# Normalised context: DMA transpose in place of TensorE transposes, with the layernorm's scale and bias moved into the weights

## What is computed

```python
xn = layernorm(ctx, ln1_w, ln1_b)          # context, 32 x 375 x 256
ln = layernorm(_layernorm(x), ln2_w, ln2_b)
q = (ln @ Wq) per head * (1 + fside) + fside
k, v = split(xn @ Wkv)                     # 16 heads of 64
out = softmax(q @ k.T / 8) @ v @ Wout
x = x + tanh(g_xattn) * out
x = x + tanh(g_ffn) * bitlinear(gelu(bitlinear(_layernorm(x), w1, b1)), w2, b2)
```

## Time and profile before

| | |
|---|---|
| median of 3 runs | 1112.73 us (1112.56 to 1113.78) |
| profiled execution, its time | 1112.75 us |
| its span, first to last instruction | 1110.3 us |
| TensorE matmul (PE) busy | 1063.3 us, 96% |
| weight loads (PEld) | 731.0 us, 66% |
| ScalarE (ACT) busy | 969.6 us, 87% |
| VectorE (DVE) busy | 943.7 us, 85% |
| GpSimd (POOL) busy | 772.5 us, 70% |
| DMA packets of the SP queue | 65.3% of 16 engines' span |

### The profile page before, as it was taken

The page is one execution under the profiler, slowest core; times in us unless marked ns, Lnnn a source line. Parts: engine busy times, 40 slices in busy tenths (PEclk is TensorE's granted clock), DMA queues, the critical chain, the costliest instruction groups (busy, mean ns, idle before and its releaser), DMA issues.

```text
span 1110.3 us, 32139 instructions
## 1 busy us (share of the span) xinstructions
PE 1063.3 (96%) x11910; PEld 731.0 (66%) x11910; DVE 943.7 (85%) x2113; ACT 969.6 (87%) x1867; POOL 772.5 (70%) x838
## 2 busy tenths in 40 slices
PE   3899999999999999999999999999999999999995
PEld 2566667666676666767667667666767667677663
DVE  5797788988888889888988878988888988888886
ACT  5887799999999889999999979999999997999873
POOL 3666667786677767676777766777676777768752
PEclk9899999999999999999999999999999999999998
DMA  8457567666767665679755676755768755765571
GB/s 272 86 106 114 94 102 135 99 110 120 116 119 127 114 101 126 115 111 130 120 98 125 117 107 119 119 101 125 111 120 124 122 98 113 118 113 122 115 124 43
DMA packets 408153, 129.08 MB, mean 116 GB/s; under 512 B 389792, under 2 KB 402848, under 8 KB 408000
## 3 DMA queue, kind: packets, MB, share of 16 engines
q1 hardware_dynamic: 408000, 127.03, 65.3%
HBM read 26.71 MB, written 3.67 MB: 27 GB/s over the span
## 4 chain that ended last, share of the span: by engine, by line
PE 75%; ACT 10%; DMA 5%; issue 4%; POOL 2%; DVE 2%; POOLq 1%; DVEq 1%; ACTq 0%
PE work L872 14%; PE work L873 13%; PE work L874 13%; PE ps_s L891 11%; DMA pt<-pn 5%; PE ps_o L872 3%; PE ps_o L874 3%; PE ps_o L873 3%; ACT prob L618 3%; ACT L618 2%; ACT q_f L584 2%; PE work L955 2%; PE work L997 2%; PE work L946 2%; PE work L968 2%
## 5 line engine op out<-in xcount | busy, mean ns | idle before, releaser
L452 POOL TENSOR_TENSOR pn<-prob,pn 112x750 f16<-112x750 f32 x256 | 399.2, 1565 | 111.5 <-ACT pn L628 100.0
L618 ACT ACTIVATE prob<-ps_s,neg_max 112x375 f32<-112x375 f32 x512 | 264.6, 572 | 10.4 <-DVE neg_max L779 8.6
L779 DVE TENSOR_REDUCE neg_max<-ps_s 112x2 f32<-112x750 f32 x256 | 237.8, 929 | 21.1 <-PE ps_s L891 21.0
L872 PE MATMUL ps_o<-v_h,pt 128*128 128x65 f16 (+1 forms) x1536 | 166.1, 194 | 10.5 <-DMA pt<-pn 8.1
L872 PE MATMUL work<-z,wkv_h 128*128 128x375 f16 x512 | 168.0, 328 | 2.7 <-POOL z L473 2.5
L701 DVE SCALAR_TENSOR_TENSOR k_l<-work,k_h 128x375 f16<-128x375 f32 x256 | 136.4, 541 | 37.9 <-ACT k_h L540 37.8
L540 ACT ACTIVATE k_h<-work 128x375 f16<-128x375 f32 x256 | 121.4, 487 | 53.0 <-PE work L874 48.6
L874 PE MATMUL work<-z,wkv_l 128*128 128x375 f16 x512 | 166.8, 326 | 0.0
L873 PE MATMUL work<-z,wkv_h 128*128 128x375 f16 x512 | 166.5, 325 | 0.0
L873 PE MATMUL ps_o<-v_l,pt 128*128 128x65 f16 (+1 forms) x1536 | 165.9, 192 | 0.0
L874 PE MATMUL ps_o<-v_h,pt 128*128 128x65 f16 (+1 forms) x1536 | 165.8, 193 | 0.0
(11 more groups left out here) (144 smaller groups left out, 2717.7 us busy)
## 6 DMA issues: line engine op xcount, KB each, us to landing
ctx_in<-in_ctx SPq DMA_DIRECT2D x32, 375.0 KB
pt<-pn SPq DMA_TRANSPOSE x256, 3.5
x_in<-in_x SPq DMA_DIRECT2D x32, 112.0 KB, 3.8
x_res<-in_x SPq DMA_DIRECT2D x28, 128.0 KB, 5.0
out<-y SPq DMA_DIRECT2D x28, 128.0 KB, 2.0
stage<-in_wkv SPq DMA_DIRECT2D x2, 1024.0 KB, 9.6
stage<-in_w SPq DMA_DIRECT2D x2, 1024.0 KB, 13.3
stage<-in_wq SPq DMA_DIRECT2D x1, 1024.0 KB, 8.7
```

The costliest lines, as they stand in the source:

```text
L452: g.tensor_tensor(buf[:, 1, :, 0:SK], prob[:, p % 2], buf[:, 0, :, 0:SK], ALU.subtract).then_inc(p_lo, 1)
L618: i = a.activation(prob[:, p % 2, h, :], ps_s[0:SQ, 2 * (p % 2) + h, 0:SK], ACT.Exp, bias=neg_max[:, 2 * (p % 2) + h:2 * (p % 2) + h + 1])
L779: v.tensor_reduce(neg_max[:, 2 * (p % 2):2 * (p % 2) + 2], ps_s[0:SQ, 2 * (p % 2):2 * (p % 2) + 2, 0:SK], X, ALU.max, negate=True).then_in ...
L872: t_.matmul(dst, sh, mh, start=(n == 0), stop=False)
```

## The change

- `Z0`, `Z1`, `ZF0`, `ZF1`, `ZS0`, `ZS1` are gone. GpSimd splits `ctx_n` as it lies, 125 rows by 768, into fp16 halves `zt` (ZC), and one DMA transpose a batch (ZD, issued by SP) turns both into `z`, now in tiles of 128 columns of which 125 are used.
- The layernorm's scale goes into the key and value weights when they are split. Its bias times the key weights (BK) becomes the bias of the key casts, KH and KL, which also lose their constant 1/64 (key weights are scaled by 8, and the query's factors are divided by 8). Its bias times the value weights (BV) times the output weights (BR) becomes one row that a matmul of ones adds in each WO.
- All three key tiles have 125 keys, so the casts and splits of the probabilities write six runs of 125.
- The four small layernorm loads are issued ahead of the key weights. `deq1` has two buffers.
- All lists are written anew. In the repeated round TensorE has:

```diff
+    ("Q0", 0), ("A2", -1), ("A3", -1), ("K5", 0), ("S7", -1), ("K6", 0), ("K7", 0), ("V02", 0),
+    ("S0", 0), ("S1", 0), ("V00", 0), ("A4", -1), ("V01", 0), ("A5", -1), ("K0", 1), ("Q1", 0),
+    ("S2", 0), ("S3", 0), ("ZX", 1), ("K1", 1), ("A6", -1), ("A7", -1), ("OO0", -1), ("V10", 0),
+    ("S4", 0), ("V11", 0), ("K2", 1), ("A0", 0), ("K3", 1), ("OO1", -1), ("S5", 0), ("S6", 0),
+    ("F0", -2), ("V12", 0), ("F1", -2), ("A1", 0), ("WO", -1), ("F2", -3), ("K4", 1),
```

GpSimd and SP:

```diff
+    ("PL2", 1), ("LNA", 3), ("ZXS", 2), ("PL3", 1), ("XB", -1), ("PL4", 1), ("ZC", 3), ("PL5", 1),
+    ("RM2", -1), ("QS0", 2), ("PL6", 1), ("PL7", 1), ("RM1", 0), ("HQ", -1), ("PL0", 2), ("QS1", 2),
+    ("PL1", 2), ("XQ", 0),
...
+    ("ST", -1), ("T4", 2), ("LX", 5), ("T5", 2), ("T6", 2), ("T7", 2), ("HD", 0), ("RS", 2),
+    ("T0", 3), ("XD", 1), ("T1", 3), ("T2", 3), ("T3", 3), ("LD", 6), ("ZD", 5),
```

The rest, cut to its core:

```diff
+            def turn_context(b):
+                sp.wait_ge(z_split, b + 1)
+                if b > 1:
+                    sp.wait_ge(full[BANK[LAST_Z_USER[b - 2]]], USE[LAST_Z_USER[b - 2]])
+                sp.dma_start_transpose(z[b % 2][:].rearrange("p a t c q -> p (a t c) q"),
+                                       zt[:].rearrange("p a t d -> p (a t d)")).then_inc(z_turned, 16)
...
+            def split_context(b):
+                pool.wait_ge(ctx_normed, b + 1)
+                if b > 0:
+                    pool.wait_ge(z_turned, 16 * b)
+                g.tensor_copy(zt[0:TP, 0], ctx_n[:])
                 pool.drain()
+                g.tensor_tensor(zt[0:TP, 1], ctx_n[:], zt[0:TP, 0], ALU.subtract).then_inc(z_split, 1)
...
+            def split_normed_hi(n, loaded, scale, w, hi_part):
+                act.wait_ge(loaded, 16)
+                for k in range(KC):
+                    i = a.activation(hi_part[:, k], w[:, k], ACT.Identity, scale=lnw1s[:, scale, k:k + 1])
...
-                    hi((name, b), job, k_h[:, int(name[2]), :], work[:, BANK[job], 0:SK])
+                    a.activation(k_h[:, c, :], work[:, BANK[job], 0:SK], ACT.Identity, bias=bias_k[:, c:c + 1]).then_inc(hi_done, 1)
...
-                    lo((f"KH{c}", b), job, k_l[:, c, :], work[:, BANK[job], 0:SK], k_h[:, c, :])
+                    v.scalar_tensor_tensor(out=k_l[:, c, :], in0=work[:, BANK[job], 0:SK], scalar=bias_k[:, c:c + 1], in1=k_h[:, c, :],
+                                           op0=ALU.add, op1=ALU.subtract).then_inc(evacuated[BANK[job]], 1)
...
-                    pe.wait_ge(z_ready, 2 * b + 2)
+                    pe.wait_ge(z_turned, 16 * (b + 1))
...
+                    i = three(w[:, 0:SK].rearrange("p (t q) -> p t q", t=TT),
+                              [(wkv_h[:, k, c], wkv_l[:, k, c], zb[:, 0, :, k, 0:TP], zb[:, 1, :, k, 0:TP]) for k in range(KC)])
...
+                if name in ("BK", "BV"):
+                    first = INNER * (name == "BV")
+                    for c in range(IC):
+                        for k in range(KC):
+                            i = t_.matmul(w[:, c:c + 1], wkv_f[:, k, first + c * P:first + (c + 1) * P], lnb1[:, k:k + 1],
+                                          start=(k == 0), stop=(k == KC - 1))
+                if name == "BR":
+                    for c in range(IC):
+                        i = t_.matmul(w[0:QUARTER + 1, 0:D], bias_v[:, c, :], wout_f[:, c, :], start=(c == 0), stop=(c == IC - 1))
...
-                if name in ("Z0", "Z1"):
-                    pe.wait_ge(ctx_normed, b + 1)
-                    c = int(name[1])
-                    for t in range(TT):
-                        i = t_.transpose(w[:, t * TP:(t + 1) * TP], ctx_n[:, t, c * P:(c + 1) * P], ident[0:TP, 0:TP])
...
+                    t_.matmul(w[:, 0:D], bias_ones[:], bias_row[:], start=True, stop=False)
                     for c in range(IC):
-                        t_.matmul(w[:, 0:D], oh, wout_h[:, c, :], start=(c == 0), stop=False)
+                        t_.matmul(w[:, 0:D], oh, wout_h[:, c, :], start=False, stop=False)
```

More of the change, by code:

```diff
@@ L224 @@
     BANK[job], USE[job] = n % WORK_BANKS, n // WORK_BANKS + 1
+FIRST_KEY_HALF = [s[0] for s in sequence("ACT") if s[0] in ("WKH0", "WKH1")][0]
 GELU_COUNT = [t + 1 if t < NT - 1 else t + 2 for t in range(NT)]
 LAST_HALVES = [int(s[0][2]) for s in sequence("DVE") if s[0] in ("HE0", "HE1") and s[1] == NT - 1]
+LAST_Z_USER = [[s for s in sequence("PE") if s[0][0] in "KV" and s[1] == b][-1] for b in range(B)]
 HI_COUNT = {s: n + 1 for n, s in enumerate(s for s in sequence("ACT") if s[0][0:2] in ("KH", "VH"))}
@@ L291, in build @@
         xc, xr, xq = sb("xc", [P, D]), sb("xr", [P, D]), sb("xq", [P, D], F16)
-        amax1, clip1, inv1, qs1, deq1 = (sb(n, [P, 1]) for n in ("amax1", "clip1", "inv1", "qs1", "deq1"))
+        amax1, clip1, inv1, qs1 = (sb(n, [P, 1]) for n in ("amax1", "clip1", "inv1", "qs1"))
+        deq1 = [sb(f"deq1_{i}", [P, 1]) for i in range(2)]
         xqt = sb("xqt", [P, KC, P], F16)
@@ L565, in step @@
                 if name[0:2] == "KH":
-                    hi((name, b), job, k_h[:, int(name[2]), :], work[:, BANK[job], 0:SK])
+                    if b == 0:
+                        act.wait_ge(evacuated[BANK["BK", 0]], USE["BK", 0])
+                    c = int(name[2])
+                    act.wait_ge(full[BANK[job]], USE[job])
+                    a.activation(k_h[:, c, :], work[:, BANK[job], 0:SK], ACT.Identity, bias=bias_k[:, c:c + 1]).then_inc(hi_done, 1)
+                if name == "BRH":
+                    job = ("BR", 0)
+                    act.wait_ge(full[BANK[job]], USE[job])
+                    a.activation(bias_row[:], work[0:QUARTER + 1, BANK[job], 0:D], ACT.Identity, scale=W_SCALE).then_inc(bias_hi, 1)
                 if name[0:2] == "OH":
@@ L585, in step @@
                     i.then_inc(evacuated[BANK[job]], 1)
-                if name in ("ZF0", "ZF1"):
-                    c = int(name[2])
-                    if b == 0:
-                        act.wait_ge(ln_in, 16 * 4)
-                    act.wait_ge(full[BANK[job]], USE[job])
-                    a.activation(zf[:, c, :], work[:, BANK[job], 0:SK], ACT.Identity, bias=lnb1[:, c:c + 1],
-                                 scale=lnw1[:, c:c + 1]).then_inc(evacuated[BANK[job]], 1)
                 if name == "ZXF":
@@ L672, in split_lo, with split_normed_lo @@
                 i.then_inc(lo_split[n], 1)
-            def split_z_first():
-                dve.wait_ge(evacuated[BANK["Z1", 0]], USE["Z1", 0])
-                v.tensor_copy(z[0][:, 0, 1], zf[:, 1])
-                dve.drain()
-                v.tensor_tensor(z[0][:, 1, 1], zf[:, 1], z[0][:, 0, 1], ALU.subtract).then_inc(z_ready, 1)
+            def split_normed_lo(n, scale, w, hi_part, lo_part, count=1):
+                dve.wait_ge(hi_split[n], count)
+                for k in range(KC):
+                    i = v.scalar_tensor_tensor(out=lo_part[:, k, :], in0=w[:, k, :], scalar=lnw1s[:, scale, k:k + 1], in1=hi_part[:, k, :],
+                                               op0=ALU.mult, op1=ALU.subtract)
+                i.then_inc(lo_split[n], 1)
             def sum_weight(n):
@@ L751, in step @@
                     c = slice(int(name[3]) * HALF, (int(name[3]) + 1) * HALF)
-                    split_lo(0, wkv_f[:, :, c], wkv_h[:, :, c], wkv_l[:, :, c], int(name[3]) + 1)
-                if name == "ZS1":
-                    split_z_first()
+                    split_normed_lo(0, 0, wkv_f[:, :, c], wkv_h[:, :, c], wkv_l[:, :, c], int(name[3]) + 1)
+                if name == "BKE":
+                    job = ("BK", 0)
+                    dve.wait_ge(full[BANK[job]], USE[job])
+                    v.tensor_scalar(bias_k[:], work[:, BANK[job], 0:IC], K_SCALE, None, ALU.mult).then_inc(evacuated[BANK[job]], 1)
+                if name == "BVE":
+                    job = ("BV", 0)
+                    dve.wait_ge(consts_ready, 3)
+                    dve.wait_ge(full[BANK[job]], USE[job])
+                    v.tensor_copy(bias_v[:, :, 0], work[:, BANK[job], 0:IC])
+                    v.tensor_copy(bias_v[:, :, QUARTER], work[:, BANK[job], 0:IC]).then_inc(evacuated[BANK[job]], 1)
+                if name == "BRL":
+                    job, row = ("BR", 0), slice(QUARTER, QUARTER + 1)
+                    dve.wait_ge(bias_hi, 1)
+                    v.scalar_tensor_tensor(out=bias_row[row], in0=work[row, BANK[job], 0:D], scalar=W_SCALE, in1=bias_row[row],
+                                           op0=ALU.mult, op1=ALU.subtract).then_inc(evacuated[BANK[job]], 1)
                 if name == "WQL":
@@ L847, in step @@
                         dve.wait_ge(small_in, 16 * 4)
-                    v.scalar_tensor_tensor(out=hid[:, c], in0=work[:, BANK[job], :], scalar=deq1[:], in1=b1_row[:, c],
+                    v.scalar_tensor_tensor(out=hid[:, c], in0=work[:, BANK[job], :], scalar=deq1[b % 2][:], in1=b1_row[:, c],
                                            op0=ALU.mult, op1=ALU.add).then_inc(evacuated[BANK[job]], 1)
@@ L922, in job @@
```

(5 more changed lines are left out.)

91 lines of the change are left out of this document (54 added, 37 removed), and 211 rows, old and new, of the table CAST_ACT.

## The result

| | median, us | lowest to highest | runs | ratio to before, 95% |
|---|---|---|---|---|
| before | 1112.76 | 1112.43 to 1113.78 | 6 | |
| after | 1108.12 | 1106.31 to 1110.76 | 6 | 0.9958 [0.9942, 0.9974] |

The change makes the kernel 4.6 us faster, 0.42%. The forecast was 1102: the sign was right, the gain less than half of the 10.7 us worked out. The profiled execution of after took 1108.29 us with a span of 1106.5.

What follows compares the result with a forecast made beforehand. TensorE was taken as the bound; its list summed to -11.6 us (-28.2 + 3.1 + 6.5 + 3.5 + 3.5), and with +1 for the start 1112.75 became 1102 us. Forecast case 1097 to 1108 (0.55), range 1095 to 1121.

Steps and rivals of the forecast that it cites:

- What bounds the kernel: Steady part: TensorE bounds it, so a microsecond off its list is worth about one, if ScalarE and VectorE keep up.
- Z0 and Z1: TensorE: removing these jobs, three fp32 transposes each, saves 0.94 us a batch, -28.2 us over 30 batches.
- The matmul in WO: TensorE: one added matmul of 256 columns in each of 28 token tiles, 0.11 us each, +3.1 us.
- Groups of scores: TensorE: score jobs stand in 160 separate groups instead of 134; 26 splits at 0.25 us cost +6.5 us.
- BV and BR: TensorE, once: 16 one-column fp32 matmuls and 8 fp32 calls of 256 columns, +3.5 us each.
- BK: TensorE, once: BV's size, but placed where TensorE waits for data anyway, so free; uncovered 3.5 us more.
- Key matmuls in runs of 125: TensorE: reading three runs of 125 columns instead of 375 in a row costs between 0 and 21 us, taken 0.
- Value weights of 125: TensorE: narrower value loads are slower, but each lies behind a matmul of 216 ns and is covered, 0 us.
- The start: First batches: 21.4 to 25 us lost, but the second hole gone; -1 to +3 us, taken +1.
- The other engines: ScalarE net 30.1 us and VectorE 30.0 a batch, both at 92% of a 32.8 us period; GpSimd's changes hidden.
- SP's queue: SP issues one more transpose a batch ahead of ST and T4; with 8 us of margin the wait costs nothing.
- rival (a): Turns come late, so A4 or A7 waits for probabilities: slower, 1123 us at 0.7 us a batch; chance 0.18.

Runs made afterwards that it cites:

- run 1: Changed kernel with bias_ones and bias_row on 128 partitions instead of 33, the added ones zero: 1104.47 us, ratio to before 0.9929.
- run 2: Changed kernel with the value jobs' weights taken 128 columns wide instead of 125, the added ones zero padding: 1104.55 us, ratio to before 0.9936.
- run 3: Changed kernel without the bias matmul in WO, so the output lacks the value bias; BK, BV, BR still run: 1100.11 us, ratio to before 0.9890.
- run 4: Changed kernel with six fp32 transposes of ctx_n added to each ZX, into columns nobody reads: 1126.13 us, ratio to before 1.0133.
- run 6: Changed kernel with OO1 put between S5 and S6 in TensorE's repeated round, so both stand alone: 1121.53 us, ratio to before 1.0084.
- run 9: Changed kernel with the bias matmul on 128 partitions and the value weights 128 columns wide: 1101.19 us, and 1100.13 us when repeated.
- run 8: Changed kernel without BV, BR, their evacuations and the bias matmul in WO, so no value bias in the output: 1098.28 us, ratio to before 0.9886.
- run 5: Changed kernel with S4 S5 together after A0 and S6 S7 together after WO, four score groups a batch for five: 1171.80 us, ratio to before 1.0540.
- run 10: Changed kernel with 128-partition bias matmul and 128-wide value weights, plus BV moved to the start right behind BK: 1102.75 us, ratio to before 0.9917.

## Why the prediction was right in sign and too large in size

- **What bounds the kernel**: right. TensorE has no idle time in a full batch, and what is taken off its list comes off the period one for one, as what is added goes on (runs 1, 2, 3, 4, 6, 9).
- **Z0 and Z1, -28.2**: right. 26.4 us in the account for all 32 batches, and the wait ahead of Z1, which the account books with the keys (0.23 less a full batch); run 4 shows 21.2 of it directly.
- **The matmul in WO, +3.1**: wrong, and the largest miss. It measured 8.6. The step that failed reads "512 columns take 0.216 us, so 256 take 0.11": that is the distance in a row of matmuls whose weights have 128 rows and are loaded ahead. The operand of 33 rows was in the code, and no row of before showed such a one. Run 1 shows the two places where it failed, 0.13 us ahead and 0.21 behind, which fall to 0.03 and 0.11 with 128 rows. It should have had bounds, not a value.
- **Groups of scores, +6.5**: right. The lists of after have 161 groups, not 160, so 27 more; 0.23 us each, 6.2 us, and 0.29 in run 6. The 2.5 us of waits and delays in and behind score jobs had no term.
- **BV and BR, +3.5 each**: right for their own time, 3.7 and 3.6; run 8 leaves open how much of it is on the path. The stretch at half clock behind BV, 1.7 us here, had no term. BK was covered, as said (13.0 to 19.9, with 1.2 us of waiting behind it).
- **Key matmuls in runs of 125, 0**: right, the matmuls stay 0.16 us apart.
- **Value weights of 125, 0**: wrong, +3.7 by the span of run 2. The step that failed reads "each lies behind a matmul of 216 ns, so either is covered". It doesn't hold for the first load of a value job after a group of scores (0.267 us to the next matmul, 0.227 with 128 columns) nor, in part, after an apply job; 393 against 381 ns are its sign in after. The Trainium skill (TensorE: Matmul & The Clock Gate, "Weight-path perf modes") gives the fast load to exactly 128 weights; this trace agrees, with 97 ns for 128 columns and 137 for 125, and the time depends on how many of them show.
- **The start, +1**: about right. With BV and BR the terms for it came to 8 us; the third batch's first scores came 4.9 us later than before, with the transposes of a batch or two fewer ahead of them. Both executions have a stretch at half clock in there, so the agreement is no finer than 2 us. The first query matmul started at 21.08, inside the 21 to 22 named.
- **The other engines**: the casts cost what was read from other rows (578 for 572, 602 for 600), and VectorE and ScalarE at 89 and 92% of the period don't set it in a full batch.
- **SP's queue and rival (a)**: the new turn costs nothing, and the waits of apply for turns went away rather than grew, 8.1 us to none. Nothing in the sum had this gain; no run separates what it comes from.

With the two corrections the sum is 1102 + 5.5 + 3.7 = 1111.2, and the measured 1108.3 of the profiled execution lies 2.9 below it. The waits for turns that went away, 8.1 us, are larger than that, so some 5 us were added elsewhere: the end of the kernel took 2.5 us more with its new orders, waits and delays in and behind score jobs 2.5. These are readings of the account; no run takes them apart.

## What to carry to other kernels

Price a new matmul by its whole operand, not by its columns alone: a bias row added by a matmul of ones belongs on 128 partitions of zeros, and a partial tile of keys on 128 columns of weights. In a kernel bound by TensorE, look at the first matmul after each change of the weights' shape, since that is where a load shows. An order written out by hand for five engines leaves little room to change one of them alone: run 5 lost 64 us, and run 6, a swap of two jobs, 13. And look up the granted clock near the start before comparing two spans.

## What the runs showed of the hardware that was not expected

- Weights of 33 rows are not loaded ahead of the matmul before, and the load after them isn't either: 0.13 + 0.21 us where 128 rows cost 0.03 + 0.11. Weights of 125 rows (the apply jobs) behave like 128. The Trainium skill (TensorE: Matmul & The Clock Gate, "LDWEIGHTS (loading the stationary operand)") says that a load of 32 rows takes as long as one of 128. That agrees with the load by itself, 93 ns against 97; the cost lay in when the load starts.
- Behind the 64-row weights of the scores a first load isn't taken ahead either: the load engine is idle for 0.28 us, and the first value load starts with its matmul. Its width then costs 0.04 us, 137 against 97 ns. A group of scores costs 0.09 us ahead of it as well, whatever the job before.
- Early in the execution matmuls run at half the pace of later ones. In run 9 key matmuls start 0.31 us apart from 22.86 to 24.74, the pace of 1.2 GHz for 375 columns, and 0.16 apart from 25.27 on, that of 2.4 GHz; the granted clock's column shows 1.00 for both stretches, so that early it can't be relied on. Before them TensorE had stood still to 12.2, done its one-column matmuls to 19.5 and waited 1.2 us. In run 10 the pace changes between 31.19 and 31.43. A job moved into the first 20 us cost 6.8 us where it had cost 3.7 at 37 us, so a hole there takes half the work that its length says. Later the column can be relied on: in after it shows 0.50 from 41.66 to 45.08, and 512-column matmuls stand 0.43 us apart there, 0.216 elsewhere.
